# A four-layer graph network on one core: ScalarE normalizes rows, queries in fp32, edge MLP products over pairs of steps

## The chip, the cores and the metric

The kernel runs on one core of one Trainium2 chip. The metric is the device time of one execution in microseconds; lower is better.

## The reference, cut to what matters

6250 nodes with 128 features, 100,000 directed edges sorted by target. Four layers follow each other, and after each the node rows are normalized (`(x - m) / sqrt(v + 1e-5)`):

```python
x = _layernorm(x + attention_gcn(...))      # layer 0: one logit per edge, weighted segment sum, a 128x128 product
x = _layernorm(x + transformer(...))        # layer 1: Q = x @ Wq, K, V; softmax over 4 heads of 32; segment sum; Wo, Wm
x = _layernorm(x + h + mlp(...))            # layer 2, with h = x:
#   e = silu(concat(h[row], h[col]) @ We1 + be1)    (100000, 64)
#   e = silu(e @ We2 + be2)                         (100000, 64)
#   agg = segment_sum(e, row); out = silu(concat(h, agg) @ Wn1 + bn1) @ Wn2 + bn2
x = _layernorm(x + gcn(gcn(...)))           # layer 3: two graph convolutions, self loops, relu between
```

All arithmetic is fp32 in the reference.

## The kernel before, in words

Nodes stand as 52 tiles of 128 rows; a node stage handles four tiles at a time, in NB = 13 batches. Edges are cut into 782 tiles of 128 edges, and each edge tile is split further wherever it crosses from one node tile to the next, which gives 832 steps. The stages run one after the other, each a block with a barrier at its end:

- preparation, with the weights loaded by SP's queue; then n0 (table of layer 0) and l0 (edges of layer 0, with a sort for layer 2 on VectorE);
- n1: finish layer 0, normalize, write the key-value table t1 and the query tile `look`; l1: edges of layer 1;
- n2: finish layer 1, normalize, write table t2 and `look2`; l2: edges of layer 2 (edge MLP);
- n3, c1 (first convolution), n4, c2 (second convolution); n5: add, normalize and write out.

**Edge stages.** GpSimd (POOL) issues one indirect DMA per edge tile or step, which fetches 128 table rows: L540 for l0 and l1 (groups of G = 4), L1676 for l2, L2027 for the convolutions (groups of CG = 8). The ring of l2 holds 12 groups, and the gathers run ahead of the consumers as far as it and `landed` (two groups in flight) allow. l2 has 98 groups of gathers and 104 groups of steps; group k of steps waits for group k of gathers while k < 98.

**A group of l2.** VectorE: `hot_look` (L1799), `before_silu` (L1810, eight adds of 64 columns, waits for the gather), `hot_sum` (L1816, one-hot rows for the sum, 1024 columns in one instruction), `add` (L1826). ScalarE: `silu1` (L1705), `keep_silu1` (L1710), second SiLU (L1718). TensorE, in this order in `step`: `own_half(k+2)` (L1744, 24 bf16 products of 64 columns), `turn(k+1)` (L1753, eight fp32 transposes of 128x64), `second_product(k)` (L1760, eight fp32 products with `we2`, 64 columns each, the bias as a 65th row), `summed(k-1)` (L1767: a product of zeros over 512 columns that opens the bank; L1772: eight fp32 products; L1774: the same product of zeros that closes it). An fp32 matmul stands in the trace as two instructions, an fp32 transpose as one. The order on each engine is the program's; `from_group` and `at_least` are waits on constants or on the loop's index.

**Queries of l1.** Each group turns its one-hot tile into bf16 (`one_hot`, L1241 and L1242), transposes it (L1284), copies it (`keep_hot`, L1246), and TensorE picks the query rows (L1293): twelve bf16 products, since the fp32 query is held as three bf16 parts in `look`. n1 makes these parts: the first by ScalarE (L1149), the rest by `rest` and `last_part` of VectorE (L1040, L1045) and `second_part` of ScalarE (L1140).

**Node stages n1, n2, n5.** VectorE adds up tile tY, takes its statistics (`norm_stats`, L573 and L577), ScalarE takes the root (`root`, L592), VectorE inverts it (L583) and writes the normalized rows, `normalize` (L586, four instructions of 128x128). In n1 and n2 TensorE then transposes them (L1112, L1547) and multiplies by the next weights. tY is one buffer. On ScalarE a batch of n1 is: root(b), copy of the transposed rows (L1145), query (L1149), two copies of keys and values (L1153, L1154), then the copy for batch b+2 (L1136). A batch of n2 is: root(b), `projected(b+1)` (L1574, which `mix(b+1)` on TensorE, L1537 and L1538, waits for), copy (L1585), and so on; TensorE does `mix(b+1)` before it transposes the rows of b. After its last batch n2 has VectorE fill the row of ones below `s1T` (L1513).

Of the kernel before, what the change touches and what calls it, by code (L numbers as in the profile page):

```python
# [16 lines left out]
F32 = mybir.dt.float32  # L17
# [7 lines left out]
P = 128  # L25
D = 128
# [66 lines left out]
def build(nc, x, edge_i, edge_f, W_att_w, W_att_b, W1_w, W1_b, W2_w, W2_b, a_vec,  # L93
# [3 lines left out]
    with ctx:  # L97
# [33 lines left out]
        look = arena[:, 0:NT * 3 * D // 2].bitcast(BF16).rearrange("p (t c) -> p t c", t=NT)  # L131
# [7 lines left out]
        dst_score = look[:, 0:NT, :].rearrange("p t c -> p (t c)").bitcast(F32)[:, 0:NP]  # L139
# [53 lines left out]
        we2 = sb("we2", [EH + 1, EH])  # L193
# [25 lines left out]
        lookf = look[:, :, :].rearrange("p t c -> p (t c)").bitcast(F32)  # L219
# [20 lines left out]
        s1T = tab_rows(2 * CG * P, EH + 1).rearrange("p (k c) -> p k c", k=2)  # L240
# [12 lines left out]
        sort_b = hotT[:, :, :].rearrange("p a b -> p (a b)").bitcast(F32)  # L253
        pre_now = hot[:, :, :, :].rearrange("p a b c -> p (a b c)").bitcast(F32).rearrange("p (k u f) -> p k u f", k=2, u=CG)
# [33 lines left out]
        with nc.Block() as block:  # L288
            @block.sync
            def _(sp):  # L290
                with nc.allow_non_contiguous_dma(reason="last dst of each tile, columns of biases"):
# [26 lines left out]
                    w(we2[0:EH, :], We2)  # L318
                    w(we2[EH:EH + 1, :], be2.rearrange("(one o) -> one o", one=1))
# [50 lines left out]
            def _(dve):  # L370
                ch = Chain(dve, prep_v)
                v.memset(tile_rows[:, :, 0, :], 0)
                v.memset(tile_rows[:, :, 1, :], PAD_DST).then_inc(rows_cleared, 1)
                dve.wait_ge(iota_made, 3)
# [205 lines left out]
        def normalize(ch, b, y, outs, std):  # L580
# [109 lines left out]
        with nc.Block() as block:  # L690
# [285 lines left out]
            def _(pe):  # L976
# [43 lines left out]
         n1_cx, n1_q_rest, n1_q1, n1_split, t1_out, t1_free, n1_copied, n1_v, n1_deg, n1_dis, n1_var, n1_std) = (sem(f"n1_{n}") for n in (  # L1020
             "hn", "c", "mixed", "prod", "prodT", "prodT_kept", "mm", "xn", "xnT", "xnT_kept", "kv_mm", "q_mm", "kv_kept", "q0",
             "c_x", "q_rest", "q1", "split", "t1_out", "t1_free", "copied", "vector", "deg", "dis", "var", "std"))
        N1 = 2 + NORM
        with nc.Block() as block:
            @block.vector
            def _(dve):
# [10 lines left out]
                def rest(b):  # L1037

                    dve.wait_ge(n1_q0, b + 1)
                    v.scalar_tensor_tensor(out=tX, in0=bank[5][:, :].rearrange("p (t d) -> p t d", t=BT), scalar=SCALE,  # L1040
                                           in1=look[:, tiles(b), 0:D], op0=ALU.mult, op1=ALU.subtract).then_inc(n1_q_rest, 1)

                def last_part(b):
                    dve.wait_ge(n1_q1, b + 1)
                    v.tensor_sub(look[:, tiles(b), 2 * D:3 * D], tX, look[:, tiles(b), D:2 * D]).then_inc(n1_split, 1)  # L1045

                def batch(b, past, left):
# [12 lines left out]
                    if past > 1:  # L1060
                        last_part(b - 2)
                    dve.wait_ge(n1_copied, b + 1)
                    if past:
                        dve.wait_ge(n1_xnT, b)
                    normalize(ch, b, tY, [tN[:, u, :] for u in range(BT)], n1_std).then_inc(n1_xn, 1)
                    if past:
                        rest(b - 1)
# [22 lines left out]
                last_part(NB - 2)  # L1090
                dve.wait_ge(n1_split, NB - 1)
                rest(NB - 1)
                last_part(NB - 1)

            @block.tensor
            def _(pe):
# [12 lines left out]
                def batch(b, past, left):  # L1109
# [5 lines left out]
                    if past:  # L1115
                        pe.wait_ge(n1_q_rest, b)
# [16 lines left out]
            def _(act):  # L1133
# [4 lines left out]
                def second_part(b):  # L1138
                    act.wait_ge(n1_q_rest, b + 1)
                    s_.copy(look[:, tiles(b), D:2 * D], tX).then_inc(n1_q1, 1)  # L1140
# [1121 lines left out]
```

## Time and profile before

| | us |
|---|---|
| median of 3 runs (lowest, highest) | 5980.8 (5976.45, 5984.49) |
| the profiled execution | 5983.38, span 5981.4 |
| mean granted TensorE clock | 0.628 |
| busy: POOL, PE, DVE, ACT | 4075.3, 3703.9, 3076.2, 1681.4 |

Times in the rows below are microseconds from the start of the span. PE is TensorE's matmuls, PEld its weight loads, DVE VectorE, ACT ScalarE, POOL GpSimd. The granted clock is a share of 2.4 GHz and takes two levels, 1.0 and 0.5.

### The profile page before, as it was taken

Reading aid. Unit: us, or ns where it says so; the run is one execution under the profiler, and the core shown is the slowest. Engines: PE = TensorE matmul, PEld = TensorE weight load, DVE = VectorE, ACT = ScalarE, POOL = GpSimd, SP = SyncE. Lnnn points to the kernel's source line nnn. Section 1 sums busy time; section 2 is a strip of 40 time slices with the busy share of each in tenths; the row PEclk is TensorE's granted clock in tenths of the full one; section 3 lists DMA queues with packets and bytes.
Section 4 is the critical chain, followed back from the end, with each engine's and each line's share of the span. In section 5 each row is a group of like instructions: output and inputs, shape, how many; then the busy total and the mean of one; then the engine's idle time right before and its main releaser. Section 6 shows DMA issues by size and latency. Waiting matters only on the chain. (4 is left out here: it accounts for less than half of the span.)

```text
span 5981.4 us, 90476 instructions
## 1 busy us (share of the span) xinstructions
PE 3703.9 (62%) x20158; PEld 3022.9 (51%) x20159; DVE 3076.2 (51%) x10705; ACT 1681.4 (28%) x5852; POOL 4075.3 (68%) x4183
## 2 busy tenths in 40 slices
PE   4344444356777777679999999545445455455452
PEld 2333333345666666568888887333333343333332
DVE  5787777666777777643333333533333343333336
ACT  2333333336777777422222222100000000000000
POOL 2677777756777777357777771477777747777773
PEclk7555555567877777865555556765665665656656
DMA  3111112212333333111111210111111111111111
GB/s 98 51 52 52 52 52 56 48 49 86 104 104 104 104 104 104 48 48 52 52 51 51 55 51 12 46 53 52 52 52 52 52 48 53 52 52 52 52 52 39
DMA packets 210751, 358.53 MB, mean 60 GB/s; under 512 B 87268, under 2 KB 123698, under 8 KB 210502
## 3 DMA queue, kind: packets, MB, share of 16 engines
q0 software_dynamic: 142944, 296.35, 18.2%
q1 hardware_dynamic: 67558, 59.16, 3.2%
q8 instruction: 119, 1.95, 0.1%
q14 instruction: 130, 1.06, 0.1%
HBM read 332.22 MB, written 26.33 MB: 60 GB/s over the span
## 5 line engine op out<-in xcount | busy, mean ns | idle before, releaser
L2027 POOL DMA_INDIRECT arena<-table_gcn,idx_now x1568 | 1499.9, 957 | 487.9 <-issue 417.8
L2074 PE MATMUL pair<-arena,hotf 128*128 x3328 | 752.4, 418 | 996.2 <-DMA arena<-table_gcn,idx_now 995.6
L2074 PEld LDWEIGHTS pair<-arena,hotf 128*128 128x128 f32 x3328 | 702.3, 321 | 1129.9 <-issue 1129.7
L540 POOL DMA_INDIRECT arena<-table_attention,idx_now x832 | 827.7, 995 | 276.6 <-issue 186.9
L540 POOL DMA_INDIRECT arena<-table_key_value,idx_now x832 | 796.2, 957 | 258.9 <-issue 220.5
L1676 POOL DMA_INDIRECT arena<-table_edge_mlp,idx_now x784 | 782.1, 998 | 243.2 <-issue 214.9
L2101 DVE TENSOR_TENSOR acc<-acc,pair 128x1024 f32 x208 | 253.9, 1221 | 1348.0 <-PE pair L2077 1347.6
L998 PE MATMUL pair<-wide,hotf 128*128 128x130 f32 x1664 | 428.1, 437 | 644.7 <-ACT wide L962 644.7
L998 PEld LDWEIGHTS pair<-wide,hotf 128*128 128x128 f32 x1664 | 366.4, 324 | 708.8 <-ACT wide L962 708.8
L2036 ACT COPY idx_now<-src_t 128x8 int32 (+1 forms) x204 | 39.3, 197 | 1885.0 <-PE pair L2077 1875.3
L2091 DVE TENSOR_SCALAR hotf<-iota,rel_now,ew_now 128x128 f32<-128x128 f32 x1664 | 454.6, 360 | 7.7 <-ACT ew_now L2041 7.7
L1772 PEld LDWEIGHTS pair<-wide,hotf 128*128 128x128 f32 x1664 | 316.7, 292 | 38.9 <-issue 38.9
L1772 PE MATMUL pair<-wide,hotf 128*128 128x64 f32 x1664 | 336.3, 385 | 0.0
L1302 PE MATMUL pair<-wide,hotf 128*128 128x132 f32 x1664 | 328.8, 358 | 8.9 <-issue 7.1
L1760 PEld LDWEIGHTS pair<-we,tab 65*128 65x128 f32 x1664 | 325.0, 298 | 4.2 <-issue 0.4
L1760 PE MATMUL pair<-we,tab 65*128 65x64 f32 x1664 | 321.3, 377 | 0.0
L1826 DVE TENSOR_TENSOR acc<-acc,pair 128x512 f32 x104 | 71.4, 686 | 446.2 <-PE pair L1774 446.1
L1369 DVE TENSOR_TENSOR junk<-pair,arena 128x512 f32<-128x512 f32 x208 | 143.8, 692 | 292.6 <-DMA arena<-table_key_value,idx_now 292.6
L1293 PE MATMUL pair<-arena,hotT 128*128 x2496 | 291.0, 273 | 1.6 <-ACT hotT L1246 1.5
L1302 PEld LDWEIGHTS pair<-wide,hotf 128*128 128x128 f32 x1664 | 277.2, 249 | 14.3 <-issue 10.9
L1810 DVE TENSOR_TENSOR hot<-pair,arena 128x64 f32<-128x64 f32 x832 | 134.2, 224 | 278.4 <-DMA arena<-table_edge_mlp,idx_now 258.2
L1710 ACT COPY tab<-pair 64x1024 f32<-64x1024 f32 x104 | 104.5, 1005 | 598.9 <-PE pair L1753 598.9
(350 smaller groups left out, 6983.7 us busy)
## 6 DMA issues: line engine op xcount, KB each, us to landing
arena<-rel_dram SPq DMA_DIRECT2D x52, 512.0 KB
arena<-table_gcn,idx_now POOLq DMA_INDIRECT x1568, 2.5
arena<-table_attention,idx_now POOLq DMA_INDIRECT x832
arena<-table_key_value,idx_now POOLq DMA_INDIRECT x832
arena<-table_edge_mlp,idx_now POOLq DMA_INDIRECT x784, 2.4
table_key_value<-arena SPq DMA_DIRECT2D x13, 512.0 KB, 2.9
table_gcn<-tab SPq DMA_DIRECT2D x26, 256.0 KB, 2.3
table_attention<-arena SPq DMA_DIRECT2D x13, 264.0 KB, 2.5
```

The source lines that it names most:

```text
L540: q_.indirect_dma_start(ring[:, slot, 0:width], None, table, bass.IndirectOffsetOnAxis(ap=idx_now[:, slot:slot + 1].bitcast(U32), axis=0)) ...
L998: last = t_.matmul(bank[2 * (g % 2) + u // 2][:, (u % 2) * AW:(u % 2) * AW + D + 2], hotf[:, g, u, :], wide[:, g, u, 0:D + 2], start=True, ...
L1293: last = t_.matmul(QB[g % 2][:, u * P:(u + 1) * P], hotT[:, g, u * P:(u + 1) * P], flat(look[:, bass.ds(nodes[u], 1), c * D:(c + 1) * D]), ...
L1302: last = t_.matmul(bank[SUM + 2 * (g % 2) + u // 2][:, (u % 2) * AW:(u % 2 + 1) * AW], hotf[:, g, u, :], wide[:, g, u, :], start=True, sto ...
L1369: ch(v.tensor_tensor(out=prod.rearrange("p (u d) -> p u d", u=G), in0=QB[g % 2][:, :].rearrange("p (u d) -> p u d", u=G), in1=ring[:, g * ...
L1676: q_.indirect_dma_start(mlp_ring[:, slot * EH:(slot + 1) * EH], None, t2, bass.IndirectOffsetOnAxis(ap=idx_now[:, slot:slot + 1].bitcast(U ...
L1760: last = t_.matmul(EB[:, u * EH:(u + 1) * EH], s1T[:, g % 2, u * P:(u + 1) * P], we2[:, :], start=True, stop=True)
L1772: t_.matmul(window[:, bass.ds(offset * EH, EH)], hot8[:, g % 2, u, :], s2[:, g % 2, u * EH:(u + 1) * EH], start=False, stop=False)
L2027: q_.indirect_dma_start(conv_ring[:, slot * D:(slot + 1) * D], None, table, bass.IndirectOffsetOnAxis(ap=idx_now[:, slot:slot + 1].bitcast ...
L2074: t_.matmul(window[:, bass.ds(offset * D, D)], hot8[:, g % 2, u, :], conv_ring[:, bass.ds(slot * D, D)], start=False, stop=False)
L2091: last = v.tensor_scalar(out=hot8[:, g % 2, u, :], in0=iota[:, :], scalar1=rel_now[:, at], scalar2=ew_now[:, at], op0=ALU.is_equal, op1=AL ...
L2101: v.tensor_add(here, here, pair[g % 4][:, :].rearrange("p (t d) -> p t d", t=CG)).then_inc(added, 1)
```

## The change

1. **Normalization.** `normalize` of n1, n2 and n5 moves from VectorE to ScalarE. `factors` on VectorE keeps the reciprocal and adds one small instruction (128x4) that makes the offset -mean/std; ScalarE then computes row * scale + offset in four activations with a scale and a bias taken from tiles. In n2 `projected(b+1)` stands ahead of `root(b)`.
2. **Queries.** `look` holds the query once, in fp32. The bf16 one-hot tile of l1 and the three-part split in n1 go; transposes are fp32, and a step's query is one fp32 product.
3. **Edge MLP in pairs.** `turn` transposes two steps at once (four transposes of 128x128), `we2` is a 128x128 block diagonal, the second product is four fp32 products of 128 columns, and the bias comes from one bf16 product (3 rows, 512 columns) in the same accumulation.
4. **Closing products.** The zeros that close an accumulation in l2, c1 and c2 cover 2 columns, not 512.

```diff
+        def factors(ch, b, std, factors_made):
             ch.eng.wait_ge(std, b + 1)
             ch(v.reciprocal(stat[:, :, 6], stat[:, :, 6]))
             ch.wait()
+            v.scalar_tensor_tensor(out=stat[:, :, 7], in0=mv[:, :, 0], scalar=-1.0, in1=stat[:, :, 6],
+                                   op0=ALU.mult, op1=ALU.mult).then_inc(factors_made, 1)
+        def normalize(act, b, y, outs, factors_made):
+            act.wait_ge(factors_made, b + 1)
             for u in range(BT):
-                last = v.tensor_scalar(out=outs[u], in0=y[:, u, :], scalar1=mv[:, u, 0:1], scalar2=stat[:, u, 6:7],
-                                       op0=ALU.subtract, op1=ALU.mult)
+                last = s_.activation(outs[u], y[:, u, :], ACT.Identity, scale=stat[:, u, 6:7], bias=stat[:, u, 7:8])
...
                 def batch(b, past, left):                      # ScalarE, n1
                     root(act, b, n1_var, n1_std)
+                    act.wait_ge(n1_copied, b + 1)
+                    if past:
+                        act.wait_ge(n1_xnT, b)
+                    normalize(act, b, tY, [tN[:, u, :] for u in range(BT)], n1_factors).then_inc(n1_xn, 1)
                     act.wait_ge(n1_xnT, b + 1)
                     s_.copy(rT[:, 1, :], bank[2][:, :]).then_inc(n1_xnT_kept, 1)
-                    if past:
-                        second_part(b - 1)
...
-                    s_.activation(flat(hotf[:, g, :, :]), away, ACT.Relu, scale=-1.0, bias=1.0)
-                    s_.activation(flat(hot[:, g, :, :]), away, ACT.Relu, scale=-1.0, bias=1.0).then_inc(l1_hot, 1)
+                    s_.activation(flat(hotf[:, g, :, :]), away, ACT.Relu, scale=-1.0, bias=1.0).then_inc(l1_hot, 1)
...
-                        for c in range(3):
-                            last = t_.matmul(QB[g % 2][:, u * P:(u + 1) * P], hotT[:, g, u * P:(u + 1) * P],
-                                             flat(look[:, bass.ds(nodes[u], 1), c * D:(c + 1) * D]), start=(c == 0), stop=(c == 2))
+                        last = t_.matmul(QB[g % 2][:, u * P:(u + 1) * P], hotT_f[:, g, u * P:(u + 1) * P],
+                                         flat(look[:, bass.ds(nodes[u], 1), :]), start=True, stop=True)
...
                 def batch(b, past, left):                      # ScalarE, n2
-                    root(act, b, n2_var, n2_std)
                     if left:
                         projected(b + 1)
+                    root(act, b, n2_var, n2_std)
...
+                ch(v.memset(ones3, 1.0))                       # end of n2: 13 small instructions that split be2 into three
+                ch(v.tensor_copy(be2_b[:, 0, :], be2b[:, :]))  # bf16 rows
...
-                v.memset(s1T[EH:EH + 1, :, :], 1.0)
...
-                    for u in range(CG):
-                        last = t_.transpose(ST[0:EH, u * P:(u + 1) * P], junk[:, g % 2, u * EH:(u + 1) * EH], ident[:, :])
+                    for u in range(CG // 2):
+                        at = slice(u * P, (u + 1) * P)
+                        last = t_.transpose(ST[:, at], junk[:, g % 2, at], ident[:, :])
...
                 def second_product(k, g):
+                    at_least(pe, l2_s2, k, 0)
+                    t_.matmul(EB, ones3, bias2, start=True, stop=False)
                     pe.wait_ge(l2_s1T_kept, k + 1)
-                    at_least(pe, l2_s2, k, 0)
-                    for u in range(CG):
-                        last = t_.matmul(EB[:, u * EH:(u + 1) * EH], s1T[:, g % 2, u * P:(u + 1) * P], we2[:, :], start=True, stop=True)
+                    for u in range(CG // 2):
+                        at = slice(u * P, (u + 1) * P)
+                        last = t_.matmul(EB[:, at], s1T[:, g % 2, at], we2[:, :], start=False, stop=(u == CG // 2 - 1))
...
-                    t_.matmul(window, zeros2[:, 0:P], zeros2, start=False, stop=True).then_inc(l2_sum, 1)
+                    t_.matmul(window[:, 0:2], zeros2[:, 0:P], zeros2[:, 0:2], start=False, stop=True).then_inc(l2_sum, 1)
...
-                            last = t_.matmul(window[:, h * 512:(h + 1) * 512], zeros[:, 0:P], zeros, start=False, stop=True)
+                            last = t_.matmul(window[:, h * 512:h * 512 + 2], zeros[:, 0:P], zeros[:, 0:2], start=False, stop=True)
```

Smaller parts: the copy L1710 is 128x512 instead of 64x1024; We2 is loaded twice and be2 as a broadcast row (one more load in the preparation, and two memsets of 64x64 on VectorE).

## Rows read from the trace of the kernel before

**Rows 1.** Windows l1, l2: length, PE, PEld, DVE, ACT, POOL busy (x), clock, DMA, GB/s
```profile
1402.00:2465.00 1063.00, 779.09 (x5616) 662.18 (x5616) 751.32 (x2910) 773.81 (x2496) 796.24 (x832) 0.77 0.35 103
2591.00:3715.00 1124.00, 1096.15 (x6888) 946.67 (x6888) 370.83 (x1147) 245.83 (x512) 783.99 (x787) 0.55 0.18 49
```

**Rows 2.** One line, the gathers of l2: ns min/median/max, first and last start
```profile
L1676 POOL DMA_INDIRECT arena<-table_edge_mlp,idx_now x784: 951/955/2002, 2591.5 to 3611.3; - x196
```

**Rows 3.** Timeline of l2 around the last gather, clock 0.5: start, us, what [idle before]
```profile
3611.54 1.88 PE L1753 MATMUL pair<-ident,junk 128*64 128x128 f32 x8
...
3613.22 3.51 PE L1760 MATMUL pair<-we,tab 65*128 65x64 f32 x16
...
3615.57 1.28 DVE L1810 TENSOR_TENSOR hot<-pair,arena 128x64 f32<-128x64 f32 x8 [4.31 <-DMA arena<-table_edge_mlp,idx_now]
...
3617.19 3.67 PE L1772 MATMUL pair<-wide,hotf 128*128 128x64 f32 x16
...
3620.80 0.60 PE L1774 MATMUL pair<-wide 1*128 1x512 bf16 x1
...
3622.64 1.89 PE L1753 MATMUL pair<-ident,junk 128*64 128x128 f32 x8
```

**Rows 4.** Timeline, c1's group after its last gather, clock 0.5, 128 columns
```profile
4812.90 3.75 PE L2074 MATMUL pair<-arena,hotf 128*128 x16 [6.19 <-DMA arena<-table_gcn,idx_now]
```

**Rows 5.** Timeline, the last instruction of l2
```profile
3705.34 0.69 DVE L1826 TENSOR_TENSOR acc<-acc,pair 128x512 f32 x1 [3.88 <-PE pair L1774]
```

**Rows 6.** Timeline of l2's third group, where TensorE is not yet behind
```profile
2623.40 1.27 DVE L1810 TENSOR_TENSOR hot<-pair,arena 128x64 f32<-128x64 f32 x8 [8.09 <-DMA arena<-table_edge_mlp,idx_now]
2624.59 0.95 POOL L1676 DMA_INDIRECT arena<-table_edge_mlp,idx_now  x1 [0.30 <-issue]
2624.59 1.25 DVE L1816 TENSOR_TENSOR hotf<-iota,rel_now 128x1024 f32<-128x1024 f32 x1
...
2625.48 1.89 PE L1753 MATMUL pair<-ident,junk 128*64 128x128 f32 x8 [3.64 <-ACT junk L1705]
```

**Rows 7.** Timeline of l2, a gather that was held
```profile
3205.28 1.22 DVE L1816 TENSOR_TENSOR hotf<-iota,rel_now 128x1024 f32<-128x1024 f32 x1
3205.34 1.98 POOL L1676 DMA_INDIRECT arena<-table_edge_mlp,idx_now  x1 [0.30 <-issue]
```

**Rows 8.** Timeline of n1, one batch
```profile
1336.84 1.11 DVE L586 TENSOR_SCALAR arena<-arena,mv,stat 128x128 f32<-128x128 f32 x4
...
1343.22 0.61 ACT L1136 COPY hotf<-pair 128x512 f32<-128x512 f32 x1
...
1344.68 0.30 ACT L592 ACTIVATE stat<-mv,eps 128x4 f32<-128x4 f32 x1 [0.85 <-DVE mv L577]
...
1345.51 1.12 DVE L586 TENSOR_SCALAR arena<-arena,mv,stat 128x128 f32<-128x128 f32 x4
```

**Rows 9.** Timeline of n2: one batch, then its end
```profile
2532.92 0.69 ACT L1574 ACTIVATE hotf<-pair,boc 128x512 f32<-128x512 f32 x1 [1.02 <-PE pair L1530]
...
2535.61 0.60 PE L1547 MATMUL pair<-ident,arena 128*128 128x128 f32 x4
...
2586.32 1.76 DVE L1513 MEMSET tab<- 1x2048 f32 x1 [0.46 <-issue]
```

**Rows 10.** Timeline of n5, one batch and the start of the next
```profile
5942.55 0.69 DVE L2191 TENSOR_TENSOR arena<-arena 128x512 f32<-128x512 f32 x1
...
5944.71 0.30 ACT L592 ACTIVATE stat<-mv,eps 128x4 f32<-128x4 f32 x1 [5.01 <-DVE mv L577]
...
5947.88 0.69 DVE L2191 TENSOR_TENSOR arena<-arena 128x512 f32<-128x512 f32 x1
```

**Rows 11.** Groups of ScalarE activations: busy, mean ns | idle before
```profile
L1241 ACT ACTIVATE hotf<-junk 128x512 f32<-128x512 f32 x208 | 128.5, 618 | 5.2 <-PE pair L1302 1.7
...
L1980 ACT ACTIVATE hotf<-pair,bn1c 128x512 f32<-128x512 f32 x13 | 8.9, 687 | 37.8 <-PE pair L1951 35.4 <-PE pair L1942 2.4
```

**Rows 12.** Timeline of l1, four activations of 128 columns with a bias taken from a tile
```profile
2104.34 1.28 ACT L1231 ACTIVATE junk<-iota,rel_now 128x128 f32<-128x128 f32 x4
```

More of the change, by code:

```diff
@@ L192, in build @@
         be1b = sb("be1b", [P, EH])
-        we2 = sb("we2", [EH + 1, EH])
+        we2 = sb("we2", [P, P])
+        be2b = sb("be2b", [P, EH])
         wn1 = sb("wn1", [P, 2, D])
@@ L317, in _ @@
                     row(be1b[:, :], be1)
-                    w(we2[0:EH, :], We2)
-                    w(we2[EH:EH + 1, :], be2.rearrange("(one o) -> one o", one=1))
+                    w(we2[0:EH, 0:EH], We2)
+                    w(we2[EH:P, EH:P], We2)
+                    row(be2b[:, :], be2)
                     w(wn1[:, 0, :], Wn1[0:D, :])
@@ L1059, in batch @@
                     norm_stats(ch, tY, n1_var)
-                    if past > 1:
-                        last_part(b - 2)
-                    dve.wait_ge(n1_copied, b + 1)
-                    if past:
[L1064 to L1067, printed above, removed]
+                    factors(ch, b, n1_std, n1_factors)
                     if left > 1:
@@ L1163, in _ @@
                 batch_rounds(act, batch)
-                second_part(NB - 1)
             @block.gpsimd
@@ L1481, in batch @@
                         last_part(b - 2)
[L1482 to L1485 removed]
+                    factors(ch, b, n2_std, n2_factors)
                     if past:
@@ L1511, in _ @@
                 v.memset(zeros2, 0.0)
+                ch = Chain(dve, n2_bias)
+                ch(v.memset(ones3, 1.0))
+                ch(v.tensor_copy(be2_b[:, 0, :], be2b[:, :]))
+                for c in range(3):
+                    ch(v.tensor_scalar(out=is_row[:, c:c + 1], in0=part[:, 0:1], scalar1=float(c), scalar2=None, op0=ALU.is_equal))
+                ch.wait()
+                for c in (1, 2):
+                    ch(v.tensor_sub(be2p[:, c, :], be2p[:, c - 1, :] if c > 1 else be2b[:, :], be2_b[:, c - 1, :]))
+                    ch.wait()
+                    ch(v.tensor_copy(be2_b[:, c, :], be2p[:, c, :]))
+                    ch.wait()
+                ch(v.tensor_scalar(out=be2p[:, 3, :], in0=be2_b[:, 0, :], scalar1=is_row[:, 0:1], scalar2=None, op0=ALU.mult))
+                for c in (1, 2):
+                    ch.wait()
+                    ch(v.scalar_tensor_tensor(out=be2p[:, 3, :], in0=be2_b[:, c, :], scalar=is_row[:, c:c + 1], in1=be2p[:, 3, :],
+                                              op0=ALU.mult, op1=ALU.add))
+                ch.wait()
+                ch(v.tensor_copy(bias2.rearrange("p (u f) -> p u f", u=CG), be2p[0:3, 3, :].unsqueeze(1).to_broadcast([3, CG, EH])))
                 dve.wait_ge(n2_rows, 32)
-                v.memset(s1T[EH:EH + 1, :, :], 1.0)
                 by_group = step2_node[:, 0:STEPS].rearrange("p (k u) -> p k u", u=CG)
@@ L2195, in batch @@
                         front(b + 1)
-                    normalize(ch, b, tY, [flat(tab[:, bass.ds(b * BT + u, 1), 0:D]) for u in range(BT)], n5_std).then_inc(n5_done, 1)
+                    factors(ch, b, n5_std, n5_factors)
                     assert ch.n == N5
@@ L2205, in _ @@
                     root(act, b, n5_var, n5_std)
+                    normalize(act, b, tY, [flat(tab[:, bass.ds(b * BT + u, 1), 0:D]) for u in range(BT)], n5_factors).then_inc(n5_done, 1)
             @block.gpsimd
```

61 lines of the change are left out of this document (28 added, 33 removed).

## Prediction

> **What bounds the kernel now.** I read the windows by stage first, since the chain of waits ends in n5 and follows only that stage. In l1 GpSimd is busy 796 of 1063 us with 832 gathers, one per 1.27 us, and TensorE has 284 us of idle time [rows 1]: the gathers set l1's pace. In l2 two engines are close: TensorE is busy 1096 of 1124 us at a granted clock of 0.55 [rows 1], and the gathers run from 2591.5 to 3611.3 [rows 2]. So I read l2 by timeline. Near its end VectorE still waits for the gather (4.31 us) before L1810 at 3615.57, but the transposes that follow (L1753) start only at 3622.64 [rows 3], 7.07 us later. In the third group, where TensorE is not behind and waits for ScalarE, the same distance is 2.08 us [rows 6]. The gathers set l2's pace up to the last of them, and TensorE sets the tail: from 3622.64 to the last instruction's end, 3706.03 [rows 3, 5], is 83.4 us. The node stages are chains with a period per batch: n1 8.67 us [rows 8], n5 5.33 us [rows 10].
>
> **Edge MLP, TensorE.** At clock 0.5, which is 1.2 GHz, the eight transposes take 1.68 us from start to start (3611.54 to 3613.22), so 0.21 each. The sixteen instructions of the product with `we2` take 3.51 us at 64 columns, and the sixteen of L1772 take 3.67 [rows 3]; the sixteen of the convolution, with 128 columns, take 3.75 at the same clock [rows 4]. So an instruction costs about 0.22 us at either width, and half the instructions cost half the time. Per group at this clock: transposes 4 x 0.21 = 0.84 saved; product 8 x 0.22 = 1.76 saved; the bias product, whose nearest row is L1774 (512 columns in one bf16 product, 0.60), costs 0.53 after overlap (bounds 0.4 and 0.6); the closing product saves between 0.4 and 0.6 of its 0.60, I take 0.45. Together 2.5 us of 11.1 (3611.54 to 3622.64). The copy L1710 gets shorter, but TensorE never waits for it.
>
> The tail holds after 3622.64 seven transposes, eight products and nine closings: 7 x 0.84 + 8 x (1.76 - 0.53) + 9 x 0.45 = 19.8 us. About a third of the groups run at clock 1.0, where the product's share is half; that takes 1.8 off: 18. To this comes the lag of 7.07 - 2.08 = 5.0 us. **Tail: -23 us** (bounds -16 and -27).
>
> **Edge MLP, gathers.** Before the last gather TensorE's faster groups buy nothing by themselves: the cover is the gathers, eight at 1.26 us (0.95 busy and 0.30 between [rows 6]), 10.1 us a group, against 8.6 on TensorE. If the cover were gone the gain would be larger, not smaller. But the gathers are not all alike. Without holds 783 steps of 1.26 us make 986.6 us; they took 1019.8 [rows 2], so 33 us went to long ones. A long one took 1.98 us, and L1816 had started 0.06 us before it [rows 7]; it ended when L1816 had ended and the rest of the gather's work was done. In the third group L1816 starts with the gather and the gather takes its 0.95 [rows 6]. So a gather is held if L1816 is already running when it starts. Where L1816 falls depends on who paces the group. When VectorE waits for the gather, L1816 starts 1.19 us after L1810 (2623.40 to 2624.59 [rows 6]), right at a gather's start; of the six groups of which this is the first, five were free and one was held by 1.05 us. When TensorE paces, it falls anywhere. After the change all 98 groups should be of the first kind: 98 / 6 = 16 holds, 16 to 17 us, against 33. **Gathers: -17 us** (bounds: no hold, -33; all held, 98 x 1.05 - 33 = +70).
>
> **Queries in fp32 (l1).** Per group ScalarE loses one 0.62 us instruction, of the kind of L1241 [rows 11]. TensorE exchanges twelve bf16 products for eight fp32 instructions, at worst 8 x 0.22 = 1.76 us at clock 0.5 [rows 3], and its four transposes cost up to 4 x 0.21. It had 284 us idle over 208 groups, 1.37 us each [rows 1], and the growth is at most about 0.9 us. The next late thing stays the gather. **0 us** (0 to +5).
>
> **Normalization on ScalarE.** Four activations with one operand from a tile take 1.28 us [rows 12]. The second such operand has no row; the first adds 687 - 618 = 69 ns [rows 11], so 4 x 0.07 more: 1.56 us (bounds 1.28 and 1.84). VectorE's four took 1.11 [rows 8]. From root to normalization is 0.83 us now [rows 8]; the new small instruction adds about 0.2 (it is one more handover inside those 0.83, which hold three).
> The Trainium skill, ScalarE: Activation LUTs, Rules for kernel authors, says that multiplications and additions belong on VectorE, which is faster per element. The rows agree for the single instruction (1.11 against 1.56), and by that rule alone 39 batches would lose 0.45 us each, 18 us. The chains below decide otherwise only where VectorE's own queue is the chain.
>
> *n5.* VectorE does everything in line. New chain: L2191 to root 2.16 (5942.55 to 5944.71 [rows 10]) + 0.83 + 0.2 + 1.56 + 0.05 = 4.80 against 5.33; 12 x 0.53 = 6.4, and the last batch is 0.65 longer. **-6** (-10 to 0).
>
> *n1.* VectorE is the chain now; it loses L586, L1040 and L1045. Next late is ScalarE's own order: root(b+1) stands behind L1136, which starts 5.27 us after the normalized rows are done (1337.95 to 1343.22 [rows 8]). With half a microsecond for L1136, 0.83, 0.2 and 1.56 the period is 8.36 against 8.67. TensorE's part now lies wholly inside this chain, so clock 0.5 hurts more than before. 12 x 0.31 less 0.65 for the last batch: **-3** (-9 to +8). Queued behind the waiting ScalarE are the copies of keys and values, and SP's write of t1 behind those.
>
> *n2.* TensorE and ScalarE alternate; VectorE has time. From L1574 to L1547 it is 2.69 us now, filled by `mix` [rows 9]. After the change the rows are ready at 0.6 (L1574) + 0.83 + 0.2 + 1.56 + 0.06 = 3.25: later than `mix` by 0.56. The swap of `projected` and `root` keeps the normalization from delaying `mix`, but the rows become the late part: 12 x 0.56 + 0.65 = 7.4. At the end the thirteen small instructions, some 0.25 to 0.3 each, replace L1513 and its wait, 2.2 us [rows 9]: +1.3. **+9** (+3 to +14).
>
> **Convolutions and preparation.** Two closings per group at up to 0.6 us are hidden up to the last gather, since TensorE waited 6.19 us for it [rows 4]; after it VectorE's add begins earlier once. **-2** for both (-6 to 0). One more load and two memsets: **+0.5**.
>
> **Sum.** -23 - 17 + 0 - 6 - 3 + 9 - 2 + 0.5 = -41.5. The profiled execution took 5983.4 us; 5983.4 - 41.5 = 5941.9. The median of the runs is 2.6 below that execution: **5939 us**.
>
> **The rivals.** (a) *L1816 locks onto the gathers from the wrong side.* If landings come only 0.05 to 0.1 us earlier, L1816 starts just before a gather in every group, as in rows 7, and each is held by 1.05 us. All 98: +70 in place of -17, **6026 us**, slower. It decides from 56 holds on; slower by 0.2% from 68. For it: the margin in rows 6 is nothing. Against: five of six early groups were free. 7%. (b) *Holds have another cause and stay at 33 us*: **5956 us**. Against it stand rows 6 and 7. 10%. The Trainium skill, SBUF — State Buffer, Who interferes with whom, speaks for (b): there tensor_tensor, which L1816 is, takes only the pair's read interface and doesn't stall descriptor writing. The trace disagrees in rows 7. (c) *No hold at all*, since the lock falls on the free side every time: **5923 us**. 15%. (d) *The second product doesn't halve*, because time goes with columns: TensorE then needs 11.1 - 0.84 - 0.45 + 0.53 = 10.3 us a group, the holds stay as they are, and the tail gains 23 - 14 = 9: -9 - 1.5, **5970 us**. Rows 3 against rows 4 speak against it. 6%. (e) *ScalarE loads tables between root and normalization*: in n5 alone 13 x 2 x some 1.3 us, **5973 us**. Against it: n2 already runs L592 and L1574 (Identity) in turn. 3%.
>
> **How the numbers follow.** The forecast has 59%. Its own range, from the tail, n1, n2 and n5, is 5925 to 5955; with (b) and (c) and a third to half of the groups held, 8 in 10 lie between 5908 and 5970. A measurement of this kernel can tell about 0.2%, 12 us, from no change. Faster by more: the forecast, (b), (c): 0.84. Within: (d), (e) and part of (a): 0.09. Slower: 0.07.
>
> **What would show it.** L1753 and L1760 with half the instructions at 0.21 and 0.22 us; the last gather of l2 starting at about 3595 less what n1 and n2 moved; some 16 gathers above 1.1 us; L1753 about 2.1 us behind L1810 all through l2; from the last gather's landing to l2's end about 71 us instead of 91; periods of 8.4 (n1), 8.45 in place of 7.9 (n2), 4.8 (n5); l1 unchanged in length. I am wrong if long gathers number over 50, or if TensorE in l2 never waits.

## The result, and the profile after

The changed kernel takes 5960.5 us (median of 20 executions, 5940.8 to 5984.1); the kernel before, 20 times beside it, 5976.6. The ratio is 0.9971, interval 0.9962 to 0.9981: 16 us faster, where 41.5 were forecast. In twelve further executions, of a later set, it was 0.9987 (0.9977 to 0.9998). The direction held and 5960 lies in the range, but the gain is less than half of the forecast. The profiled execution, at 5940.8 against a predicted 5941.9, would have hidden that: it was the fastest of the 20.

The page's first lines, and the windows of l1 and l2 (length, busy time of PE, PEld, DVE, ACT, POOL, clock, DMA share, GB/s), which answer to [rows 1]:

```profile
span 5938.7 us, 84532 instructions
...
PE 3473.7 (58%) x18182; PEld 2853.8 (48%) x18183; DVE 3017.3 (51%) x10576; ACT 1589.6 (27%) x5787; POOL 4048.1 (68%) x4183
...
1400.00:2460.00 1060.00, 772.79 (x4778) 680.43 (x4779) 749.92 (x2904) 661.92 (x2287) 795.87 (x832) 0.86 0.35 103
2597.00:3702.00 1105.00, 1001.38 (x5851) 808.02 (x5852) 388.45 (x1207) 217.18 (x527) 769.67 (x797) 0.52 0.18 49
```

In l2 TensorE is now idle for 104 us where it was for 28, and l1 is as long as before. The gathers of l2 (ns min/median/max, first and last start), in the first profile of the changed kernel and in two more, answer to [rows 2]:

```profile
L1685 POOL DMA_INDIRECT arena<-table_edge_mlp,idx_now x784: 951/955/2002, 2597.0 to 3596.7; - x196
L1685 POOL DMA_INDIRECT arena<-table_edge_mlp,idx_now x784: 951/956/1859, 2601.1 to 3602.2; - x196
L1685 POOL DMA_INDIRECT arena<-table_edge_mlp,idx_now x784: 951/955/1996, 2603.8 to 3608.1; - x196
```

999.7, 1001.2 and 1004.3 us from first to last, against 1019.8. Since single executions differ, I compare stages over several profiles: two of the kernel before (5983.4, 5970.0 us) and four of the changed one (5940.8, 5963.5, 5962.1 and 5976.5, the last from `after_3`). Every stretch runs from the first or last start of a stage's gathers to the next such start; the part behind c2's last gather is split at the first start of L2191 (L2204 after the change).

| stretch, mean us | before | after | measured | forecast |
|---|---|---|---|---|
| start to l0's first gather | 159.6 | 160.2 | +0.6 | +0.5 |
| l0's gathers | 1085.3 | 1082.1 | -3.2 | 0 |
| n1 (last gather of l0 to first of l1) | 152.6 | 159.3 | +6.7 | -3 |
| l1's gathers | 1048.1 | 1048.5 | +0.4 | 0 |
| n2 (same way) | 141.1 | 150.0 | +8.9 | +9 |
| l2's gathers | 1018.0 | 1002.2 | -15.8 | -17 |
| l2's tail and n3 | 209.5 | 192.2 | -17.3 | -23 |
| c1's and c2's gathers | 1975.9 | 1976.2 | +0.3 | 0 |
| c1's tail and n4 | 78.4 | 78.2 | -0.1 | -1 |
| c2's tail | 35.4 | 32.3 | -3.1 | -1 |
| n5 | 70.8 | 77.3 | +6.5 | -6 |
| sum | | | -16.1 | -41.5 |

The stretches add up to 16 us, as the two medians do. l0, which the change leaves alone, differs by 3 us, within the spread of single executions. So the forecast failed in n1 (by 10), n5 (by 12) and l2's tail (by 6).

### The profile page after: what moved, and what is told of

Same layout as the page of the kernel before. It is cut to its first block and busy times, and to the rows that moved or that the text cites. A ratio compares the mean times of both kernels' runs of the same rounds, so it can differ in the third digit from the quotient of the medians.

```text
span 5938.7 us, 84532 instructions
## 1 busy us (share of the span) xinstructions
PE 3473.7 (58%) x18182; PEld 2853.8 (48%) x18183; DVE 3017.3 (51%) x10576; ACT 1589.6 (27%) x5787; POOL 4048.1 (68%) x4183
## 5 line engine op out<-in xcount | busy, mean ns | idle before, releaser
L1685 POOL DMA_INDIRECT arena<-table_edge_mlp,idx_now x784 | 762.0, 972 | 244.4 <-issue 212.1
L1013 PEld LDWEIGHTS pair<-wide,hotf 128*128 128x128 f32 x1664 | 369.5, 326 | 697.5 <-ACT wide L977 697.5
L1822 DVE TENSOR_TENSOR hot<-pair,arena 128x64 f32<-128x64 f32 x832 | 134.0, 225 | 637.5 <-DMA arena<-table_edge_mlp,idx_now 624.4
L1784 PEld LDWEIGHTS pair<-wide,hotf 128*128 128x128 f32 x1664 | 353.0, 323 | 44.2 <-issue 44.2
L1784 PE MATMUL pair<-wide,hotf 128*128 128x64 f32 x1664 | 372.2, 416 | 0.0
L1292 PE MATMUL pair<-wide,hotf 128*128 128x132 f32 x1664 | 301.0, 336 | 10.6 <-issue 9.2
L1283 PE MATMUL pair<-arena 128*128 x1664 | 282.8, 327 | 2.0 <-ACT arena L1237 2.0
L1283 PEld LDWEIGHTS pair<-arena 128*128 128x128 f32 x1664 | 268.9, 245 | 2.9 <-issue 2.9
L1223 ACT ACTIVATE junk<-iota,rel_now 128x128 f32<-128x128 f32 x832 | 265.8, 390 | 10.6
L977 ACT ACTIVATE wide<-arena,small 128x129 f32<-128x129 f32 x832 | 267.0, 393 | 0.0
L1292 PEld LDWEIGHTS pair<-wide,hotf 128*128 128x128 f32 x1664 | 252.6, 230 | 16.0 <-issue 13.4
L889 DVE SCALAR_TENSOR_TENSOR junk<-iota,rel_now,arena 128x128 f32<-128x128 f32 x832 | 260.1, 349 | 0.0
```

The lines of the kernel that those rows point to most:

```text
L889: last = v.scalar_tensor_tensor(out=junk[:, 0, u * P:(u + 1) * P], in0=iota[:, :], scalar=rel_now[:, g * G + u:g * G + u + 1], in1=dst_sco ...
L977: last = s_.activation(wide[:, g, u, 0:D + 1], ring[:, g * G + u, 0:D + 1], ACT.Identity, scale=small[:, g, u:u + 1])
L1013: last = t_.matmul(bank[2 * (g % 2) + u // 2][:, (u % 2) * AW:(u % 2) * AW + D + 2], hotf[:, g, u, :], wide[:, g, u, 0:D + 2], start=True, ...
L1223: last = s_.activation(away[:, u * P:(u + 1) * P], iota[:, :], ACT.Abs, scale=-1.0, bias=rel_now[:, g * G + u:g * G + u + 1])
L1283: last = t_.matmul(QB[g % 2][:, u * P:(u + 1) * P], hotT_f[:, g, u * P:(u + 1) * P], flat(look[:, bass.ds(nodes[u], 1), :]), start=True, s ...
L1292: last = t_.matmul(bank[SUM + 2 * (g % 2) + u // 2][:, (u % 2) * AW:(u % 2 + 1) * AW], hotf[:, g, u, :], wide[:, g, u, :], start=True, sto ...
```

## The experiments

**The changed kernel again, twice** (edit: none). What varies from one execution to the next?

> The changed kernel once more, unaltered, for a second profile. The first one ran 5940.8 us, the fastest of 20 executions whose median is 5960.5. Theory L (lock): what differs between executions is how many gathers of l2 are held by the one-hot instruction of VectorE; the profile at hand had 33 gathers above 1.05 us, 13.5 us in all. This one should show the same lengths of n1, n2, n5 and l2's tail within 2 us each, and a number of long gathers in l2 that accounts for its time: at 5960, some 30 us in holds in place of 13. Rival T (TensorE's clock): the difference lies in l2's tail and in n1 and n2, by the granted clock there, and the gathers of l2 take the same 1000 us from first to last. Rival S: it lies in l0, whose sort on VectorE also held gathers (23 to 29 us).

> The changed kernel once more, unaltered, for a third profile. Theory L: holds in l2 between 10 and 60 us, and over the three profiles the time moves with them, us for us, n1, n2, n5 and the tail of l2 being the same within 2 us each. Rival T: the times move with the granted clock, in n1, n2 and the tail. Rival S: they move with l0.

Measured 5963.5 and 5962.1 us. The holds of l2's gathers are 14.5 and 17.0 us, against 13.5 in the first profile: theory L falls, the holds are steady. l0 differs by 2 to 3 us. Of 22.8 us between the first profile and this one, 6.5 lie in l2's tail and 8.4 between c1's last gather and c2's first; the rest is spread. Windows of that last stretch, in the first profile and in `again_1` (columns as above; how often each engine ran stands in brackets):

```profile
4811.00:4821.00 10.00, 6.89 (x51) 5.61 (x50) 8.03 (x13) 2.75 (x4) 0.00 (x0) 1.00 0.36 108
4821.00:4831.00 10.00, 6.89 (x52) 5.64 (x50) 7.93 (x12) 2.75 (x4) 0.00 (x0) 1.00 0.35 108
```
```profile
4824.00:4834.00 10.00, 8.17 (x35) 7.37 (x36) 5.26 (x9) 1.60 (x3) 0.00 (x0) 0.50 0.26 79
4834.00:4844.00 10.00, 7.67 (x32) 6.46 (x32) 6.17 (x9) 2.06 (x3) 0.00 (x0) 0.50 0.25 76
```

The same work: 51 or 52 matmuls in 10 us at a granted clock of 1.00, 32 to 35 at 0.50. From c1's last gather to c2's first the mean clock is 0.89 in the first profile (70.6 us) and 0.74 in `again_1` (79.0 us); it is 0.71 in `again_2` (80.3) and 0.67 in `after_3` (83.1). So rival T is right in kind, but its clock acts in n4, which it had not named, and n1 and n2 differ by 1.6 and 0.8 us. Why the clock falls sooner in one execution than in another stays open.

**The hold, taken away.** The one-hot rows in eight short instructions:

```diff
-v.tensor_tensor(out=hot8[:, g % 2, :, :], in0=iota..., in1=rel_now..., op=ALU.is_equal).then_inc(l2_same, 1)
+for u in range(CG):
+    last = v.tensor_scalar(out=hot8[:, g % 2, u, :], in0=iota[:, :], scalar1=rel_now[:, g * CG + u:g * CG + u + 1],
+                           scalar2=None, op0=ALU.is_equal)
+last.then_inc(l2_same, 1)
```

> The changed kernel, with the one-hot rows for the sum in l2 made by eight instructions of 128 columns with a per-partition scalar (as the convolutions make theirs, 0.37 us each) in place of one of 1024 columns with two tensors (1.22 us). Theory L: an instruction of 0.37 us can hold a gather by 0.25 us at most; the holds of l2 fall from 13.5 us in the profile at hand, and some 33 in a median execution, to under 5 us, the first to the last gather takes 987 to 992 us, the median is 25 to 35 us below that of the changed kernel (5925 to 5935) and the executions agree better than its 43 us from lowest to highest. Rival T: holds are no more than the 13 us that the profile shows; 13 us less, and the same spread. Rival V: VectorE has 1.8 us more a group, and the sums come later: 0 to 20 us slower.

```profile
L1829 DVE TENSOR_SCALAR hotf<-iota,rel_now x832: 266/279/517, 2636.5 to 3670.9; 128x128 f32<-128x128 f32 x167
L1685 POOL DMA_INDIRECT arena<-table_edge_mlp,idx_now x784: 951/955/1213, 2603.4 to 3601.0; - x196
```

The longest gather is 1.21 us where it was 2.00, and the gathers take 997.6 us, 4.6 less than the mean of the changed kernel. The time is 5965.6 us, ratio 0.9990 (0.9980 to 0.9999): no gain that can be told from the changed kernel's 0.9971 and 0.9987. Its last stretch of l2, 196.5 us, lies within the changed kernel's own 187.1 to 196.7. So shorter instructions shorten the holds, 6.7 us of them against 13.5 to 17.4, and that is worth some 5 us in one profile. 6.0 of the 6.7 stand in 41 gathers that start while another instruction of VectorE is running, the bf16 one of `hot_look` (L1811, 0.48 us). The 25 to 35 us of theory L aren't there.

**The hold, made worse.** Six adds to a spare tile ahead of the eight:

```diff
+for u in range(6):
+    v.tensor_add(spare[:, g % 2, u, :], LB[g % 2][:, u * EH:(u + 1) * EH], be2b[:, :])
 for u in range(CG):
     last = v.tensor_add(pre_now[:, g % 2, u, :], ...)
```

> The changed kernel with six more adds of 64 columns in each group of l2, ahead of the eight that wait for the gathers; their results go to a spare tile and are not used. They put the start of the one-hot instruction some 0.9 us later behind the landing, so that it runs when the next gather starts. Theory L: where it started 0.05 us behind a gather's start it now starts 0.95 behind, 0.31 ahead of the next, and holds that one by 1.22 + 0.83 - 0.955 - 0.31 = 0.78 us; in most of 98 groups, so 55 to 75 us in holds, and the time is 40 to 60 us above the changed kernel's, near 6010. Rival C (cover): 0.9 us more of VectorE in a group of 10.1 us is hidden, as VectorE waits for the gathers: within 5 us of the changed kernel.

```profile
3014.23 0.96 POOL L1686 DMA_INDIRECT arena<-table_edge_mlp,idx_now  x1 [0.30 <-issue]
3014.79 1.21 DVE L1831 TENSOR_TENSOR hotf<-iota,rel_now 128x1024 f32<-128x1024 f32 x1
...
3015.49 1.34 POOL L1686 DMA_INDIRECT arena<-table_edge_mlp,idx_now  x1 [0.30 <-issue]
...
3024.10 1.21 DVE L1831 TENSOR_TENSOR hotf<-iota,rel_now 128x1024 f32<-128x1024 f32 x1
...
3024.70 1.44 POOL L1686 DMA_INDIRECT arena<-table_edge_mlp,idx_now  x1 [0.30 <-issue]
```

5998.3 us, ratio 1.0042 (1.0027 to 1.0058), 35 us above `again_1` and 33 above `hot_eight`, on the same chip. 88 gathers are held, 42.3 us in all; the gathers take 1028.8 us. The hold follows the rule, only the delay was 0.6 us, not 0.9: a gather that starts 0.60 us after L1831 lasts 1.44 (1.21 + 0.83 - 0.60 = 1.44). All but one of the 88 start while L1831 is running, and each of these fits this sum within 0.06 us. So do the held gathers of the changed kernel's profiles, all but at most one in each. So rival C falls: a delay of 0.6 us a group on an engine that is idle for 65% of l2 cost 27 us in the gathers, by where it lies. Most of the rest isn't of l2: the stretch of l2's tail and n3 took 207.1 us against 192.2, but l2's part of it 77 against 75, and n3, which is the same in both, 130 us at a clock of 0.72 against 117 at 0.88.

**A slower chip.** The next four ran on a chip where the kernel before takes 7395.2 us.

> The kernel before once more, unaltered, for a second profile, since the one at hand (5983.4 us) is 7 us above the median of 20 executions. Theory N (node stages mis-sized): its n1 (from l0's last gather to l1's first) is again 152 us within 2, n2 141, the end from c2's last gather 106, against 159, 150 and 109.5 in three profiles of the changed kernel. What differs from its first profile lies in l0 and in the stretches after the last gathers of l2 and c1. Rival B (luck of one profile): n1 of the kernel before is really nearer 159, and the 8 us of loss there are the first profile's accident.

> The changed kernel with the first part undone: VectorE normalizes the rows again in n1, n2 and n5, and n2's root stands ahead of the projected copy, as before; queries, edge MLP and closing products stay changed. Theory N (ScalarE's normalization costs in all three stages): n2's period goes back from 8.36 to 7.89 us and the stage from 150 to 142; n5's from 5.84 to 5.33, the end from 109.5 to 103; n1, which has lost the query's splitting, gets shorter than it ever was, 140 to 150 us against 159. Together 25 to 33 us below the changed kernel: 5928 to 5935, ratio to the kernel before about 0.993. Rival K (clock): n1's length is set by TensorE's granted clock, whoever normalizes, and stays at 155 to 160: then 14 us, 5946.

> The changed kernel, with one wait in n5 altered: GpSimd's add for the next batch waits until VectorE has made scale and offset, not only until the statistics are done. In the profile VectorE's small instruction (128x4, two inputs from tiles) took 1.02 us in n5, ending with GpSimd's 1.43 us instruction that had started 0.44 us before it, and 0.17 us in n1. Theory P (GpSimd's instruction holds it): it takes 0.17 us, n5's period is 5.84 - 0.85 = 4.99 us, and the end of the kernel is 10 us shorter: 5950. Rival Q (the instruction is slow in n5 for another reason, or GpSimd's add comes too late for the sum of the next batch): it stays at 1 us, or L2204 waits for GpSimd, and the period stays at 5.8.

> The changed kernel with VectorE normalizing in n1, n2 and n5 again, and GpSimd's add of n5 moved: it waits only for VectorE's sum of this batch, so it runs beside the statistics (which read one tile) and is over before the normalization. Theory P: VectorE's four normalizing instructions fall from 1.74 to 1.11 us a batch; the period of n5 is 5.33 - 0.63 = 4.70 us, 8 us less than with the normalization moved back alone: 5920 to 5928, the fastest so far. Rival Q: no instruction of VectorE gets shorter, or its statistics get longer by as much: the same as that kernel within 3 us.

The edits: in `norm_back_2` VectorE's `normalize` of before in n1, n2 and n5; in the other two, n5:

```diff
 # n5_order_2, GpSimd
-pool.wait_ge(n5_var, b + 1)
+pool.wait_ge(n5_factors, b + 1)
 # best1_2, GpSimd; VectorE normalizes in n1, n2 and n5
-pool.wait_ge(n5_var, b + 1)
+pool.wait_ge(n5_v, N5 * b + 2)
```

The times in the expectations don't apply. Measured: 7181.3 us, ratio 0.9700 (0.9686 to 0.9714), for `norm_back_2`; 7189.4, 0.9719 (0.9704 to 0.9735), for `n5_order_2`; 7178.2, 0.9698 (0.9682 to 0.9715), for `best1_2`. What the change brings here, 3%, is in the last section. The periods in the node stages are as on the other chips, but n1 as a whole is longer by 4 to 8 us, its first batch starting that much later. The unaltered changed kernel did not run here, so the price of n5's new order is read from its period, not from the time. VectorE's small instruction in n5, in the changed kernel, and with the new order:

```profile
5887.14 1.43 POOL L2224 TENSOR_TENSOR arena<-x_nodes,bg 128x512 f32<-128x512 f32 x1 [4.41 <-DVE mv L587]
5887.58 1.02 DVE L595 SCALAR_TENSOR_TENSOR stat<-mv,stat 128x4 f32<-128x4 f32 x1
...
5888.73 1.65 ACT L602 ACTIVATE tab<-arena,stat 128x128 f32 x4 [1.52 <-DVE stat L595]
```
```profile
7134.73 0.17 DVE L595 SCALAR_TENSOR_TENSOR stat<-mv,stat 128x4 f32<-128x4 f32 x1
7135.03 1.65 ACT L602 ACTIVATE tab<-arena,stat 128x128 f32 x4 [0.67 <-DVE stat L595]
7135.16 1.27 POOL L2224 TENSOR_TENSOR arena<-x_nodes,bg 128x512 f32<-128x512 f32 x1 [3.85 <-DVE stat L595]
7135.22 1.76 DVE L2199 TENSOR_TENSOR arena<-arena,dis 128x512 f32<-128x512 f32 x1 [0.32 <-issue]
```

It took 1.02 us and ended with GpSimd's instruction (5888.60 and 5888.57); out of its way it takes 0.17. Now L2199, which took 0.68, waits for GpSimd in its place and takes 1.76, but beside ScalarE's four, where it costs almost nothing: the period goes from 5.84 to 5.11 us. Theory P holds. Its number was 4.99: L2199 now ends 0.3 us after ScalarE's last, and the next sum waits for it.

**On a chip like the first.**

> The kernel before once more, unaltered. The chip of the last four runs takes 24% longer for every kernel in the gather-bound stages (7395 us for this one), so the stage lengths of the kernel before are wanted a second time on a chip like the first. Theory N (ScalarE's normalization costs 7 to 8 us in n1): n1 is 152 us within 2. Rival B (the first profile was lucky in n1, since a batch takes 11 us instead of 8.7 where TensorE's clock falls): 155 to 160 us, as the 160.3 on the slower chip; then n1 cost next to nothing and the missing microseconds lie elsewhere.

> The changed kernel, unaltered, in rounds with the two below. On a chip like the first: 5955 to 5965, ratio to the kernel before 0.997. On the slower chip: near 7200, ratio 0.973.

> The changed kernel with VectorE normalizing again in n1, n2 and n5 (the first part of the change undone), now in rounds with the changed kernel. The profile of this kernel on the slower chip had n1 153 us (changed kernel 159), n2's period 7.89 (8.36), n5's 5.32 (5.84). Theory N: 6 + 6 + 7 = 19 us below the changed kernel, 5941, whichever chip. Rival K (clock): the faster VectorE leaves TensorE no better a clock, and n1 gives back what it gains: 12 us.

> As norm_back_3, and GpSimd's add of n5 starts behind VectorE's sum, beside the statistics. On the slower chip its n5 had a period of 4.80 us against 5.32. 12 x 0.52 = 6 us below norm_back_3, 25 below the changed kernel, 5935. If the gain is given back to the clock or the gathers, the same as norm_back_3.

The kernel before took 5978.9 us in 17 executions beside these.

| | us (median) | ratio, interval | n1 | n2 | c2's tail | n5 |
|---|---|---|---|---|---|---|
| `before_3` | 5970.0 | one execution | 153.5 | 141.1 | 35.3 | 70.9 |
| `after_3` | 5970.3 | 0.9987 (0.9977 to 0.9998) | 159.4 | 151.4 | 32.4 | 77.4 |
| `norm_back_3` | 5942.2 | 0.9934 (0.9922 to 0.9946) | 148.6 | 142.6 | 34.9 | 70.9 |
| `best1_3` | 5934.9 | 0.9926 (0.9914 to 0.9939) | 145.3 | 142.8 | 31.8 | 63.8 |

`before_3` puts n1 at 153.5: rival B falls, n1 really lost 7 us. `norm_back_3` is 28 us below the changed kernel, 9 more than expected. Its profiled execution is 33 us below that of `after_3`; n1, n2 and n5 account for 10.8, 8.8 and 6.5 of these, together 26; c2's tail took 2.5 back, and the rest is spread. Rival K falls as well. `best1_3` has the lowest median, 44 us below the kernel before. The two intervals overlap, so its 7 us over `norm_back_3` aren't clear of noise by the times; n5's length, 63.8 against 70.9, and its period show them. Its n5, where GpSimd's add lies beside the statistics and VectorE's normalization takes 1.11 us, with a period of 4.78:

```profile
5889.94 0.87 DVE L583 BATCH_NORM_STATS2 stat<-arena 128x6 f32<-128x128 f32 x4
5890.18 1.27 POOL L2231 TENSOR_TENSOR arena<-x_nodes,bg 128x512 f32<-128x512 f32 x1 [3.51 <-DVE arena L2212]
...
5892.25 1.11 DVE L604 TENSOR_SCALAR tab<-arena,mv,stat 128x128 f32 x4 [0.15 <-DVE stat L601]
```

## Why the prediction failed where it did

**Normalization, n5** (forecast -6, measured +6.5). The step "the new small instruction adds about 0.2" failed. It was priced by its size and its place in the chain, not by what runs beside it: GpSimd's add starts when the statistics are done, and VectorE's instruction, with two inputs from SBUF, waits until it ends. That is 0.85 us a batch; from root to normalization it is 1.81 us in place of 1.03. ScalarE's four and the handover behind them take 1.86 in place of 1.61: the second operand from a tile costs 0.09 us (an instruction takes 479 ns with two and 386 with one), not 0.07, since the two instructions of [rows 11] differ in their source as well, and the handover takes 0.2, not 0.05. Together 5.84 where 4.80 was worked out. The clue was in the profile of before: VectorE's normalization took 1.11 us in n1 [rows 8], and in n5, after GpSimd's add had started, 1.74:

```profile
5944.94 1.44 POOL L2210 TENSOR_TENSOR arena<-x_nodes,bg 128x512 f32<-128x512 f32 x1 [3.88 <-DVE mv L577]
...
5945.50 1.74 DVE L586 TENSOR_SCALAR tab<-arena,mv,stat 128x128 f32 x4 [0.15 <-DVE stat L583]
```

So VectorE was already paying 0.6 us there, and `best1_3` gets it back without ScalarE. The Trainium skill, SBUF — State Buffer, Who interferes with whom, says that a VectorE instruction with two SBUF inputs contends with a GpSimd instruction that reads SBUF; the trace agrees, 1.02 against 0.17 us.

**Normalization, n1** (forecast -3, measured +6.7). The period was worked out at clock 1.0, 8.36 us, and there it was right: 8.25. The step that failed is to take that clock for all 13 batches. Two batches of the changed kernel's first profile, 1331.59 to 1341.51 and 1349.76 to 1358.01:

```profile
1331.59 1.65 ACT L602 ACTIVATE arena<-arena,stat 128x128 f32<-128x128 f32 x4 [0.53 <-DVE stat L595]
...
1335.61 3.57 PE L1117 MATMUL pair<-wkv,hotf 128*128 128x256 f32 x8
...
1339.22 0.59 ACT L1146 COPY arena<-pair 128x512 f32<-128x512 f32 x1 [2.71 <-PE pair L1117]
```
```profile
1349.76 1.65 ACT L602 ACTIVATE arena<-arena,stat 128x128 f32<-128x128 f32 x4 [0.54 <-DVE stat L595]
...
1353.79 1.89 PE L1117 MATMUL pair<-wkv,hotf 128*128 128x256 f32 x8
1355.72 0.58 ACT L1146 COPY arena<-pair 128x512 f32<-128x512 f32 x1 [1.03 <-PE pair L1117]
```

L1117 takes 1.7 us more at clock 0.5 (windows over the two batches show 0.83 and 1.00), and ScalarE waits for it in line, so the batch takes 9.92. In every profile five or six of the twelve periods are 9.9 to 11.3 us, and the mean is 9.32 to 9.45. In the kernel before, VectorE was busy for 8.1 of 8.67 us beside TensorE, so a slower TensorE cost less; batches with some low clock took 9.2 us in its first profile (the first batch 10.6) and 8.9 to 10.5 in `before_3`, and the means are 8.85 and 9.08. Measured against batches at the high clock, the low clock adds 14.1 us to the twelve periods of the changed kernel, 5.4 to those of the kernel before. Without it they are 3.3 us shorter than before, near the 3.7 that were worked out. What follows the last normalization is 1.2 us longer, not 0.65. I had written that clock 0.5 would hurt more, and left it in the bound (+8) instead of the sum. With VectorE normalizing and the query's splitting gone (`norm_back_3`), the period is 7.86 at the high clock.

**Normalization, n2** (+9, measured +8.9). Right by its steps: the period was to be 8.45 and is 8.36, and ScalarE's four end 0.06 us before the transposes start, after TensorE has done `mix`. The thirteen small instructions at the end cost 1.3 us, as `norm_back_3`, which keeps them, shows.

So the three node stages lost 22 us, 1.3 of them to the edge MLP's bias. Undoing the first part gains 26 us in them (`norm_back_3` against `after_3`). The Trainium skill, ScalarE: Activation LUTs, Rules for kernel authors, which gives multiplications and additions to VectorE, would have made it 18 us slower by the rows' 0.45 us a batch; I set it aside for chains that gained more on paper than they did. The runs agree with its direction; what they show as the price are chains, VectorE's wait in n5 and ScalarE's in n1, more than the longer instruction.

**Edge MLP, tail** (-23, measured -17.3). The lag went as forecast. At the last gather L1763 starts 2.09 us behind L1822, as in 75 to 77 of the first 98 groups of each profile; in the others it is 2.3 to 4.6:

```profile
3606.19 1.28 DVE L1822 TENSOR_TENSOR hot<-pair,arena 128x64 f32<-128x64 f32 x8 [7.79 <-DMA arena<-table_edge_mlp,idx_now]
...
3608.28 1.09 PE L1763 MATMUL pair<-ident,junk 128*128 128x128 f32 x4 [2.00 <-ACT junk L1714]
```

The group went from 11.1 to 9.14 to 9.35 us at clock 0.5, not to 8.6. One group of `again_1`, against [rows 3]:

```profile
3617.43 1.09 PE L1763 MATMUL pair<-ident,junk 128*128 128x128 f32 x4
3618.45 0.60 PE L1768 MATMUL pair<-tab 3*128 3x512 bf16 x1
3618.98 2.08 PE L1772 MATMUL pair<-we,tab 128*128 128x128 f32 x8
3620.99 0.60 PE L1779 MATMUL pair<-wide 1*128 1x512 bf16 x1
3621.52 3.67 PE L1784 MATMUL pair<-wide,hotf 128*128 128x64 f32 x16
3625.13 0.18 PE L1786 MATMUL pair<-wide 1*128 1x2 bf16 x1
3625.24 1.58 PE L1753 MATMUL pair<-arena,hotT 128*128 x24
3626.71 1.09 PE L1763 MATMUL pair<-ident,junk 128*128 128x128 f32 x4
```

From start to start a transpose of two steps takes 1.02 / 4 = 0.255 us and an instruction of the product 2.01 / 8 = 0.25, where I had taken 0.21 and 0.22 from 64 columns and from the convolution. This is the step that failed: I took an instruction's time to be the same at either width. It saves 0.66 and, with the bias, 0.97 us a group, not 0.84 and 1.23; the bias at 0.53 and the closing at -0.42 were right. Over seven transposes and eight products this makes 3.3 us of the 6 missing, and nearly all that l2 itself lacks: from its last gather to the end of its last add it took 94.7 and 94.6 us before and 68.3, 76.6, 76.8 and 79.6 after, 19.4 less in the mean. The other 2.1 us stand in n3, the rest of this stretch, which the change doesn't touch. It takes 114.8 us at a clock of 0.90, in both profiles of before and in `again_2`, and 117.0 to 118.9 at 0.88 and 0.87 in the other three. Its windows in the first profile of the changed kernel and in `phase_late` hold the same 418 matmuls:

```profile
3665.00:3783.80 118.80, 85.82 (x418) 53.10 (x418) 74.85 (x201) 32.52 (x68) 29.93 (x40) 0.87 0.10 29
```
```profile
3707.80:3837.60 129.80, 96.86 (x418) 65.45 (x418) 75.00 (x201) 32.45 (x68) 30.00 (x40) 0.72 0.09 27
```

That the clock makes these 2 us is read from the profiles, not tried.

**Edge MLP, gathers** (-17, measured -15.8). The sum is right by luck; its make-up isn't. Instead of 16 holds of 1.05 us there are 33 to 37 that make 13.5 to 17.4 us. The groups locked to the gathers were free but for one in the first profile, the one-hot instruction starting between 0.03 us before and 0.17 after a gather. The step that failed is that a group in which VectorE waits for its gather meets the next gather's start five times in six, as in [rows 6]: in 32 of the 33 held gathers of the first profile VectorE had waited so. In 16 of them, as in 16 groups of each of the four profiles, a pause of 0.3 us stands among its adds or behind them, and the one-hot instruction starts 1.5 us behind L1822, not 1.2, so that it still runs when the next gather starts:

```profile
2689.23 0.97 DVE L1822 TENSOR_TENSOR hot<-pair,arena 128x64 f32<-128x64 f32 x6 [6.43 <-DMA arena<-table_edge_mlp,idx_now]
...
2690.50 0.37 DVE L1822 TENSOR_TENSOR hot<-pair,arena 128x64 f32<-128x64 f32 x2 [0.29 <-issue]
2690.79 1.22 DVE L1828 TENSOR_TENSOR hotf<-iota,rel_now 128x1024 f32<-128x1024 f32 x1
...
2691.66 1.17 POOL L1685 DMA_INDIRECT arena<-table_edge_mlp,idx_now  x1 [0.30 <-issue]
```

In 15 of the other 16 L1822 itself starts 2.9 to 4.7 us behind its group's last gather, where 2.5 to 2.8 is usual. What delays these landings, and what the pause is, stays open. Rivals (a), all held, and (c), none held, didn't occur, and (b) falls, since the holds halved and `phase_late` raised them to 42.3 us. (d) falls with the product at 2.01 us a group where it took 3.5, though width costs something, 0.25 against 0.22 us; (e) falls, as n5 has no table load. What the Trainium skill, SBUF — State Buffer, Who interferes with whom, infers, that tensor_tensor leaves descriptor writing alone, is against L1831 in `phase_late`, behind which the gathers last 1.34 and 1.44 us in place of 0.96; the measurement decides.

**Queries, convolutions, preparation.** l1 is unchanged within 0.4 us. c2's tail gained 3 us, c1's nothing, where 2 were forecast for both. The closings aren't shown as the cause of the 3: with the same 138 matmuls up to VectorE's last add, c2's tail takes 32.4 us at a clock of 0.79 before, 29.4 at 0.85 after, and 32.0 at 0.73 in `norm_back_3`, which has the short closings too. Taken together the parts other than normalization were to bring about 40 us, and `norm_back_3`, which holds just these, is 37 us (by the medians) to 39 (by the ratio) faster than the kernel before. Some 4 of these are its shorter n1, so that the sum comes nearer than its parts.

## What to carry to other kernels

An operation's price is set by what runs beside it: before adding even a 128x4 instruction to VectorE, look at what GpSimd reads from SBUF at that moment. When a step moves to another engine and two chains become one, sum the chain at TensorE's low clock too, and weight both by how often the old profile shows each clock. And when executions differ by 40 us, compare stages over several profiles; the one at hand can agree with a forecast by luck.

## What the runs showed of the hardware

On one chip the kernel before takes 7395 us instead of 5977, and the changed one (but for n5's wait) gains 2.8%. Lines of l1, kernel before, on that chip:

```profile
2405.45 0.95 POOL L540 DMA_INDIRECT arena<-table_key_value,idx_now  x1 [0.30 <-issue]
...
2407.67 0.63 ACT L1241 ACTIVATE hotf<-junk 128x512 f32<-128x512 f32 x1 [6.11 <-remote]
2407.83 0.28 DVE L1390 TENSOR_REDUCE top<-pair 1x1 f32<-1x128 f32 x1 [4.57 <-remote]
...
2411.23 0.95 POOL L540 DMA_INDIRECT arena<-table_key_value,idx_now  x1 [4.83 <-ACT idx_now L528]
```

From 2403.3 to 2407.7 TensorE, VectorE and ScalarE all stand still for something that isn't one of the program's operations; then the gathers wait 4.8 us for ScalarE's copy. The waits of l1, ScalarE's of that kind in the kernel before and in `n5_order_2` (us in total, times, longest):

```profile
ACT hotf L1241 <- remote: 499.9, 94, 6.6
```
```profile
ACT hotf L1233 <- remote: 264.8, 68, 6.5
```

The gathers of l1 take 1549 us there and 1427 after the change, those of l2 1347 and 1257. So "hidden behind the gathers" holds on one chip and not on the other, and the changed kernel, which has fewer instructions (84,532 against 90,476), gains more where the engines stop like this. Whether it gains by that was not tested. The fetching of instructions would be a guess for the stops, but the trace doesn't bear it out: from 1710 to 3190 us, nearly all of l1, the DMA queues marked instruction moved no packet, and over the whole run their packets are as many as on the other chip (119 and 130). What stops the engines, and why on this chip, stays open.
